# A two-layer transformer block on one core: when the second expert layer's first weights are fetched, and three small moves around it

## The reference

```python
logits = xt @ gate_w.T
scores = softmax(logits)
top_scores, sel = top_k(scores, 2)
routed_in = xt[token_idx] * top_scores_sorted[:, None]      # rows scaled BEFORE the expert
for e in range(8):
    h = silu(xe @ w1[e]) * (xe @ w3[e])
    out_routed += where(m, h @ w2[e], 0)
hs = silu(xt @ w1s) * (xt @ w3s)                            # shared expert
out = (hs @ w2s).at[token_idx].add(out_routed)
```

## Time and profile before

| | |
|---|---|
| median of three runs | 777.23 us (771.81 to 777.64) |
| the profiled execution | 775.64 us |
| its span in the trace | 773.9 us |
| PE busy | 707.7 us (91%) |
| DVE busy | 569.9 us (74%) |
| ACT busy | 484.7 us (63%) |
| POOL busy | 335.9 us (43%) |
| mean granted clock of PE | 0.979 |

### The profile page before, as it was taken

How to read it: one execution, slowest core, us unless ns; L and a number is a source line. 1 busy time by engine, 2 the same in 40 slices (tenths; PEclk the granted TensorE clock), 3 DMA queues, 4 the chain that set the end, 5 groups by cost and what they waited for, 6 DMA issues and landing times.

```text
span 773.9 us, 13974 instructions
## 1 busy us (share of the span) xinstructions
PE 707.7 (91%) x4957; PEld 626.4 (81%) x4957; DVE 569.9 (74%) x1004; ACT 484.7 (63%) x827; POOL 335.9 (43%) x320
## 2 busy tenths in 40 slices
PE   5798999889999999999999999999888799988884
PEld 5566777667999989998999898999777468888773
DVE  6776657466967868886878786868668877776747
ACT  2467476444567757776767676767557946776741
POOL 9456566512034323333332433132134766777440
PEclk9899999999999999999999999999989999999998
DMA  5000022027777868886867896877430577888728
GB/s 187 1 0 1 1 82 70 15 89 269 248 217 190 293 178 262 235 281 184 263 200 238 252 268 192 264 231 210 116 91 3 197 239 212 256 252 259 248 105 290
DMA packets 60406, 139.02 MB, mean 180 GB/s; under 512 B 6929, under 2 KB 30482, under 8 KB 60338
## 3 DMA queue, kind: packets, MB, share of 16 engines
q1 hardware_dynamic: 49106, 117.67, 45.6%
q0 software_dynamic: 11232, 20.46, 12.2%
HBM read 115.29 MB, written 22.81 MB: 178 GB/s over the span
## 4 chain that ended last, share of the span: by engine, by line
PE 57%; DVE 17%; DMA 8%; ACT 7%; issue 5%; POOL 4%; SPq 1%; POOLq 0%; DVEq 0%; ACTq 0%
PE ps L351 51%; DVE w_lo L1293 7%; DMA wr<-in_w1gu 5%; ACT w_hi L858 3%; POOL p_lo L732 2%; PE ps L2320 1%; DVE h_lo L1293 1%; PE ps L2276 1%; DVE x_a L1310 1%; DMA xnb<-y_d 1%; DMA xm_d<-xnb 1%; ACT h_hi L858 1%; DVE hf L1692 1%; DVE x_all L1933 1%; DVE q_lo L1293 1%
## 5 line engine op out<-in xcount | busy, mean ns | idle before, releaser
L1293 DVE TENSOR_TENSOR w_lo<-wr,w_hi 128x1024 fp32r<-128x1024 f32 (+1 forms) x192 | 219.4, 1156 | 51.0 <-ACT w_hi L858 45.8
L858 ACT ACTIVATE w_hi<-wr 128x1024 fp32r<-128x1024 f32 (+1 forms) x192 | 190.7, 997 | 14.3 <-DMA wr<-in_w1gu 11.7
L751 POOL DMA_INDIRECT x_d<-ye,sca x39 | 74.2, 1903 | 244.5 <-ACT ye L1021 205.0
L351 PE MATMUL ps<-xe_hi,w_hi 128*128 128x256 f32 x600 | 172.1, 287 | 1.3 <-DVE xe_lo L1293 1.3
L351 PE MATMUL ps<-xe_hi,w_lo 128*128 128x256 f32 x608 | 171.7, 283 | 0.0
L351 PE MATMUL ps<-xe_lo,w_hi 128*128 128x256 f32 x600 | 169.7, 283 | 0.0
L351 PE MATMUL ps<-w_hi,h_hi 128*128 128x256 f32 x422 | 124.4, 295 | 7.7 <-DVE h_lo L1293 6.0
L351 PE MATMUL ps<-w_lo,h_hi 128*128 128x256 f32 x422 | 119.2, 282 | 0.0
L351 PE MATMUL ps<-w_hi,h_lo 128*128 128x256 f32 x422 | 119.1, 282 | 0.0
L351 PEld LDWEIGHTS ps<-xe_hi,w_hi 128*128 128x128 f32 x600 | 114.9, 192 | 5.1 <-DVE xe_lo L1293 4.3
L351 PEld LDWEIGHTS ps<-xe_hi,w_lo 128*128 128x128 f32 x608 | 116.5, 192 | 0.1
(11 more groups left out here) (346 smaller groups left out, 1411.7 us busy)
## 6 DMA issues: line engine op xcount, KB each, us to landing
wr<-in_w SPq DMA_DIRECT2D x144, 512.0 KB, 4.8
wr<-in_w1gu SPq DMA_DIRECT2D x24, 512.0 KB, 4.9
wr<-in_w1d SPq DMA_DIRECT2D x24, 256.0 KB, 3.3
xn_d<-xnb SPq DMA_DIRECT2D x8, 512.0 KB, 3.5
x_all<-in_x SPq DMA_DIRECT2D x4, 512.0 KB, 5.9
x_d<-x_all SPq DMA_DIRECT2D x4, 512.0 KB, 4.9
x_all<-x_d SPq DMA_DIRECT2D x4, 512.0 KB, 4.3
xm_d<-xnb SPq DMA_DIRECT2D x4, 512.0 KB, 3.6
```

What stands on the lines that cost most here:

```text
L351: return nc.tensor.matmul(out, w, x, start=start, stop=stop, skip_group_check=True)
L751: pool.indirect_dma_start(dst, bass.IndirectOffsetOnAxis(ap=sca[n][:, col + half:col + half + 1], axis=0), ye[:, t % 2, half, :], None, co ...
L858: return s.activation(o, i, ACT.Copy)
L1293: return v.tensor_tensor(o, a, b, ALU.subtract)
```

## The change

Four edits, all at this seam:

1. In `place`, the three instructions that make `eid` become the function `experts_of_tiles`. In layer one it is called where they stood; in layer two behind the last one-hot.
2. SP's wait for `eid` and the read of its first entry move from between the fifth and the sixth store to behind the eighth.
3. SP waits there for all stores to have landed (`xn_st`, 64 x 4) before it issues the first expert weights.
4. PE's list: `transpose1(0)` goes ahead of the gate half of `shared(1, 1)`; its up half goes behind `gate_up1(0)`; `shared_down(0, 0)` goes ahead of the wait and the turns of tile 1.

```diff
             store_scaled(1, 1)
-            sp.wait_ge(r1["eid"], at(r1, "eid") + 1)
-            e_first = first_expert()
             store_scaled(2, 0)
             store_scaled(3, 1)
             store_scaled(2, 1)
+            sp.wait_ge(r1["eid"], at(r1, "eid") + 1)
+            e_first = first_expert()
+            sp.wait_ge(xn_st, 64 * NG)
             load1(0, e_first)
...
-                link(v.tensor_tensor(cmp_s[:, :, :, :], tile_b[:, :, :, :],
...
-                v.tensor_scalar(eid[n][:, :], eid_f[0:1, :], -float(E - 1), None, ALU.add).then_inc(r["eid"], 1)
+                def experts_of_tiles():
...
+                if not n:
+                    experts_of_tiles()
                 v.tensor_scalar(from_e[:, :], cum_b[:, 0, :], float(FT), None, ALU.mult)
...
                     v.tensor_tensor(ohb[:, c, :, :, :], places(P), turned_row(sb_f[:, c, :], P), ALU.is_equal).then_inc(r["hot"], 1)
+                if n:
+                    experts_of_tiles()
...
             pe.wait_ge(r1["tab"], at(r1, "tab") + 2)
+            transpose1(0)
             shared(1, 1, range(1))
-            transpose1(0)
-            shared(1, 1, range(1, 2))
             pe.wait_ge(nb["lo"], KC)
             gate_up1(0, T0)
+            shared(1, 1, range(1, 2))
+            shared_down(0, 0)
             pe.wait_ge(shf_ok, KC * 2)
             transpose1(1)
-            shared_down(0, 0)
             shared_down(0, 1)
```

More of the change, by code:

```diff
@@ L1583, in place @@
                                           n_b[:, :, :].rearrange("p k e -> p (k e)"), 0.0, ALU.mult, ALU.add))
-                link(v.tensor_tensor(cmp_s[:, :, :, :], tile_b[:, :, :, :],
-                                     cum_b[:, :, 0:E - 1].rearrange("p k (o e) -> p k o e", o=1
-                                                                    ).to_broadcast([P, 2, T0, E - 1]), ALU.is_ge))
-                link(v.tensor_reduce(eid_f[:, :], cmp_s[:, :, :, :].rearrange("p k t e -> p t k e"), AX.XY, ALU.add))
-                v.tensor_scalar(eid[n][:, :], eid_f[0:1, :], -float(E - 1), None, ALU.add).then_inc(r["eid"], 1)
+                def experts_of_tiles():
+                    link(v.tensor_tensor(cmp_s[:, :, :, :], tile_b[:, :, :, :],
+                                         cum_b[:, :, 0:E - 1].rearrange("p k (o e) -> p k o e", o=1
+                                                                        ).to_broadcast([P, 2, T0, E - 1]), ALU.is_ge))
+                    link(v.tensor_reduce(eid_f[:, :], cmp_s[:, :, :, :].rearrange("p k t e -> p t k e"), AX.XY, ALU.add))
+                    v.tensor_scalar(eid[n][:, :], eid_f[0:1, :], -float(E - 1), None, ALU.add).then_inc(r["eid"], 1)
+                if not n:
+                    experts_of_tiles()
                 v.tensor_scalar(from_e[:, :], cum_b[:, 0, :], float(FT), None, ALU.mult)
```

## The result

| | before | changed |
|---|---|---|
| median | 777.4 us (771.8 to 777.6, 4 runs) | 784.7 us (780.8 to 786.5, 4 runs) |
| ratio | | 1.0101, 95% interval 1.0057 to 1.0145 |
| profiled execution | 775.64 us | 780.83 us |
| its span | 773.9 us | 779.1 us |

A forecast was written before the change was run, and what follows sets the result against it. Bound by a chain of waits: last store, tile 0's gather, PE's work to `gate_up1(1)`, then the weights loop. Delays of 1.3 + 3.3 + 0.5 = 5.1 us on 775.64 gave 780.7 us; 8-in-10 range 775.5 to 785.5.

The forecast's parts named there:

- the sum: Forecast delay at the seam, carried through `gate_up1(1)` to the end: 1.3 + 3.3 + 0.5 = 5.1 us later.
- eid moves: VectorE's `eid` behind the last one-hot and SP's read of it behind the stores: each worth 0.
- what comes late into `gate_up1(0)`: Tile 0's weights, held for the stores, land 2.7 us later, so `gate_up1(0)` starts 1.3 us later.
- low clock: PE near tile 0's product: a low stretch costs 1.6 us, twice that at most; 0.5 us taken.
- up half in series: Between `gate_up1(0)` and `gate_up1(1)`: the moved half delays ACT's gate and DVE's product, 9.8 us for 6.5, 3.3 more.
- `shared_down(0, 0)` ahead of tile 1's turns: PE's list before `gate_up1(1)`: it and tile 1's turns fit in beside ACT and DVE, adding 0.
- The faster loop: Rival: the loop's eight weight landings quicken from 5.09 us, deciding at 4.45; at 4.0, 772 us; chance 0.06.
- No difference: Rival: slack in PE's tile work or the gather swallows the delay; 0 to 2 us remain, 776 to 777.5; chance 0.14.
- The stores as before: Rival: last store still lands at about 621.5, weights at 626.2; 5.8 us later, 781.4; chance 0.15.
- The slower case: Rival: low clock hits tile 0's product and the weights land late; above 785; chance 0.10.
- I am wrong if: Weights land before 624.2, tile 0's `hf` does not wait for the up half, or `gate_up1(1)` is late without the end following.
- the two waits of PE: Sign in the profile after: PE waits over 1 us ahead of `gate_up1(0)` and of `gate_up1(1)`, the latter at about 640.

The follow-up runs named there:

- e1: The changed kernel with PE's list as it was before; eid moves, SP's order and the wait for the stores stay; ratio to before 1.0029, 777.96 us.
- e8: The changed kernel with PE's list as before and all expert weights waiting for tile 0's gather instead of the stores; 779.6 us in a single execution.
- e5: The kernel before with only the two eid moves (VectorE's list, SP's read), no wait for stores, PE's list as before; ratio 1.0008.
- e2: The kernel before with only PE's new list, SP and DVE as before; ratio 1.0073, 781.07 us.
- e3: The changed kernel with `shared_down(0, 0)` back behind tile 1's turns, the up half still behind `gate_up1(0)`; ratio to before 1.0093.
- e6: The kernel before with only the up half of `shared(1, 1)` moved behind `gate_up1(0)`; ratio 1.0092, 782.7 us.
- e4: The changed kernel without SP's wait for the stores ahead of the first weights; ratio to before 1.0071, 779.8 us.
- e7: The changed kernel with ten idle products in PE's wait ahead of tile 0's turns; ratio to before 1.0107.
- e10: The kernel before with ACT's first shared-expert gate behind the second scaling of group 1, plus the eid moves; ratio 0.9997.
- e9: The kernel before with ACT's first shared-expert gate moved behind the second scaling of group 1, so the fifth store is issued sooner; ratio 1.0028.

## Why the prediction came out, and which step of it did not

The end does follow `gate_up1(1)`, within 1.5 us: from there to the end it is 138.7 us before, and 137.2 to 138.4 in the changed kernel and e1 to e8. The 9.2 us at that point, beside the 5.1 of the sum:

| term of the sum | forecast | shown | by |
|---|---|---|---|
| eid moves | 0 | 0 | e5 |
| what comes late into `gate_up1(0)`: the weights (forecast), the gather (shown, at the turns) | 1.3 | 1.7 | turns at 12.0 for 10.3; e1, e8 |
| low clock | 0.5 | 1.7 | turns to product 3.45 for 2.12, product 0.3 longer; e1, e2 |
| up half in series | 3.3 | 4.0 | 7.5 for 3.5 us from product's end on: e3, e6 |
| `shared_down(0, 0)` ahead of tile 1's turns | 0 | 1.8 | 9.3 for 7.5 us: changed kernel against e3, e2 against e6 |
| sum | 5.1 | 9.2 | |

e1 (3.4 us later than before) and e2 (7.5) add up to more than 9.2, for each has the low-clock stretch of 1.7 us and the changed kernel has it once.

- **Right:** that PE's list is most of it. It was the largest term, and e2 alone shows 7.5 of distance and 1.0073 of time, e1 without it 3.4 and 1.0029. Right in kind: `gate_shared(1, 1)` and `gated(1)` hold `tile1(0)` (DVE idles 6.24 us ahead of that product in the changed kernel, 6.1 to 6.6 in e2 to e4), and the stores land 0.7 us sooner when no weights stand behind them (4.4 in the changed kernel, e1, e3, e7 and e8; 4.8 in e4, e5 and e10; 5.1 to 5.2 in the kernel before, e2, e6 and e9). `hf` of tile 0 came 7.6 us behind the start of `gate_up1(0)`, forecast 7.2.
- **The step that failed** is the sentence "`shared_down(0, 0)`, half or less of the 3.5 us between 631.68 and 635.19, fits in beside ACT and DVE, and so do tile 1's turns". I compared durations and left out its own wait. It waits for `normed_lo(3)`, which DVE reaches only behind the product that the moved up half delays; and tile 1's turns stand behind it. PE sat 2.70 us in that wait (changed kernel, e2, e4, e7), and 1.8 us of it count at `gate_up1(1)`. The up half's own term was 0.7 us short as well. In e3, 4.58 us pass from the up half to the first down product, where the sum had 4.2 for its way through ACT's gate and VectorE to the end of `normed_lo(3)`; and PE's two down products, 2.94 us in series behind it, end later than the 2.6 us of VectorE's work that the sum put there.
- **Near in size, wrong in what ended it:** the 1.3 us, shown 1.7. I took the weights to end last, landing 2.7 us later; they landed 1.5 us later, and ACT, which was to find tile 0's turns waiting, still waited 1.99 us for them. The gather ended last: it was to land "by perhaps 626 to 627", 9.7 to 10.7 behind the last store, and landed at 11.9. SP's new wait puts the issue of all four first loads (1.5 MB) within 2.5 us of the gather's. e8 takes them away and the gather is at 2.8 us again; in e1 and e3 it took 5.3 and 5.6, in e4 and e5, with the weights issued 2.0 us sooner, 4.1 and 3.0. The wait thus protects the stores, worth 0.7 us against the kernel before, and exposes the gather, which costs 2.4.
- **Mis-sized:** the clock, 0.5. The price was right (1.6 us if a low stretch falls there: 1.5 to 1.7 shown, in the changed kernel, e1 to e4, e6 and e7), the weight was not. A second stretch at 0.50, the lower of the two levels, came in all of these, where PE had idled 2.4 to 4.9 us ahead of the turns (e6: 0.67 and then 1.46 us), and in e8, where it idled 6.57 us behind them. It did not come there in the kernel before, e5, e9 or e10, where that wait was 0.7 to 1.0 us. That is one execution of each, so the two are shown to go together and no more. The changed kernel's stretches:

```profile
613.60:618.90 5.30, 4.60 (x16) 2.35 (x15) 3.78 (x11) 1.38 (x3) 1.03 (x1) 0.57 0.66 210
...
622.00:626.00 4.00, 1.36 (x5) 1.25 (x6) 2.83 (x4) 2.01 (x5) 3.39 (x3) 0.83 0.90 319
626.00:630.00 4.00, 4.00 (x17) 2.38 (x16) 1.29 (x2) 1.30 (x2) 3.09 (x4) 0.75 0.72 235
```

  The half ahead of `gate_up1(0)` took 2.57 us (625.52 to 628.09), where one at full clock takes 1.72. What the change would cost with the clock held is not shown, as e7 did not hold it.
- **The rivals.** The faster loop: its eight landings were 5.1 us on average again (5.04, 4.89, 4.61, 5.24, 5.27, 5.38, 5.49, 5.08), the deciding point was 4.45. No difference: nothing is swallowed, the end came as late as `gate_up1(1)` did to 0.3 us. The stores as before: they landed 0.72 us sooner. That rival had the ring order of the Trainium skill ("DMA: Bandwidth & Descriptors", queues, rings and completion order) behind it: in ring order, what is queued behind a store should hardly hold it. The page gives the order alone; that nothing behind a store holds it was my reading of it. The measured landings of 4.44, 4.8 and 5.2 us, with the first weights issued 4.6 us or more, 2.6 or 0.65 us behind the store, are against that reading, and the measurement decides. The slower case, both clock and landing wrong, comes nearest to what happened, though the late landing was the gather's.
- **The signs.** Of "I am wrong if" none came, one of them narrowly: the weights landed 8.1 us behind the last store, which is 624.4 on the scale of before, and the bound was 624.2. Of the two waits of PE only that ahead of `gate_up1(1)` came (1.20 us); the one ahead of `gate_up1(0)` did not, and the waits of 2.82 us for the gather and 2.70 us in `shared_down(0, 0)` stood there instead. The latter is in none of the signs.

What stays open: what sets the last store's landing beside the weights, as issuing the fifth store sooner does not shorten it (e9); why the gather took 4.14 us in e4 and 2.97 in e5; and how much of the 7.3 us between the medians is luck of layer one's clock.

## What to carry to other kernels

When a step is moved ahead of another on an in-order engine, write down its first wait before its duration: the step costs the whole time to that wait's release, and everything queued behind it pays. Work that another engine's list needs ahead of its next tile belongs early, even if the engine that does it seems to have something more urgent. And a wait that spares one transfer a collision starts the held transfers at one moment: ask which transfer starts then. When an effect is 1% and layer one's clock alone moves an execution by 3.7 us, compare traces by distances from a mark just ahead of the change, not by spans.

## What the runs showed of the hardware that I had not expected

A gather of 256 rows of 1 KB landed 2.8 us after its second issue when the nearest loads (768 KB) had been issued 2.3 to 2.9 us before (kernel before), and 5.2 to 6.1 us when 1.5 MB of loads had been issued within the 2.5 us around it (changed kernel, e1, e3, e7). The first two loads, of 512 and 256 KB, took SP's queue 1.14 and 1.05 us to issue when the first came 0.65 us behind the last of three stores, and 0.36 us each when it came 2.6 or 4.6 us behind it. And the first 512 KB load, issued 0.16 us after the last store had landed, landed itself in 3.46 us, where the 24 before had a minimum of 3.8. That the queue was empty does not explain it: in e8, issued 5.2 us after that store's landing, it took 3.79.
